# Fused decoder layer: casts and layer-norm scaling moved between engines, with a new instruction order

## The reference, cut to what matters

```
x = layernorm(x + linear_attention(x))        # 16 heads of 64; q' = exp(q Wqf), k' = exp(k Wkf), 32 features
                                              # out = q' (k'^T v) / (q' sum(k') + 1e-6), then Wproj
x = layernorm(x + cross_attention(x, ctx))    # 16 heads of 8, softmax over 64 keys, then Wo
x = layernorm(x + ffn(x))                     # h = gelu(x Wfc^T); layernorm(h) w + b; h Wproj^T
                                              # Wfc, Wproj ternary: sign(W/g) min(round(|W/g|), 1), g = mean|W|
```

## Time and profile before

| | us |
|---|---|
| median of 3 runs (lowest, highest) | 662.33 (658.06, 664.6) |
| the profiled execution | 662.33 |
| its span, first to last instruction | 660.5 |
| PE busy, of the span | 619.8 |
| DVE busy | 510.0 |
| ACT busy | 422.6 |
| POOL busy | 440.5 |

### The profile page before, as it was taken

How to read it: one execution, slowest core, us unless ns; L and a number is a source line. 1 busy time by engine, 2 the same in 40 slices (tenths; PEclk the granted TensorE clock), 3 DMA queues, 4 the chain that set the end, 5 groups by cost and what they waited for, 6 DMA issues and landing times.

```text
span 660.5 us, 31376 instructions
## 1 busy us (share of the span) xinstructions
PE 619.8 (94%) x13568; PEld 450.4 (68%) x13568; DVE 510.0 (77%) x1312; ACT 422.6 (64%) x746; POOL 440.5 (67%) x606
## 2 busy tenths in 40 slices
PE   9789999999999999999999999999999998996675
PEld 6567766677767867676677767777777676675453
DVE  2654657778888879798988878997888887689577
ACT  4445475776667576866667675867766675962353
POOL 3433245768787777877787877778687876666543
PEclk9989999999999999999999999999999999998598
DMA  8011314454454647455444546374544544522401
GB/s 340 25 35 42 98 44 103 71 131 74 139 77 101 121 76 161 77 141 72 135 74 124 96 99 138 76 158 64 143 71 135 87 101 97 100 51 74 112 3 48
DMA packets 116010, 64.63 MB, mean 98 GB/s; under 512 B 94305, under 2 KB 100834, under 8 KB 115746
## 3 DMA queue, kind: packets, MB, share of 16 engines
q1 hardware_dynamic: 115874, 62.64, 42.4%
HBM read 17.01 MB, written 4.19 MB: 32 GB/s over the span
## 4 chain that ended last, share of the span: by engine, by line
PE 77%; DMA 7%; DVE 6%; ACT 4%; POOL 3%; issue 2%; SPq 1%; POOLq 0%; DVEq 0%; ACTq 0%
PE bank L337 16%; PE bank L327 9%; PE bank L357 6%; PE bank L449 4%; DMA x2T<-x2s 4%; PE bank L284 3%; PE bank L318 3%; PE bank L435 2%; PE bank L295 2%; PE bank L483 2%; PE bank L276 2%; PE bank L278 2%; PE bank L277 2%; PE bank L286 2%; PE bank L285 2%; PE bank L306 2%
## 5 line engine op out<-in xcount | busy, mean ns | idle before, releaser
L337 PE MATMUL bank<-Mh,GT 128*32 128x128 f32 x4096 | 126.4, 275 | 0.0
L337 PEld LDWEIGHTS bank<-Mh,GT 128*32 128x32 f32 x4096 | 108.6, 110 | 20.4 <-issue 18.2
L543 ACT ACTIVATE Cb<-bank 128x512 f32<-128x512 f32 x99 | 57.6, 599 | 40.0 <-PE bank L337 39.6
L867 DVE TENSOR_REDUCE mx<-bank 128x8 f32<-128x512 f32 x128 | 79.1, 680 | 3.9 <-PE bank L414 3.9
L327 PE MATMUL bank<-kp,xs 64*128 64x512 f32 x256 | 81.5, 626 | 0.0
L674 ACT ACTIVATE gall<-bank 128x512 f32<-128x512 f32 x64 | 36.3, 594 | 70.1 <-PE bank L484 69.9
L543 ACT ACTIVATE GT<-bank 128x512 f32<-128x512 f32 x110 | 59.2, 607 | 31.4 <-PE bank L327 27.6
L647 ACT ACTIVATE PT<-bank 128x512 f32<-128x512 f32 x128 | 66.8, 639 | 8.5 <-PE bank L435 8.3
L1044 POOL TENSOR_TENSOR rstd<-ve,mhalf 128x4 f32<-128x4 f32 x64 | 66.1, 1033 | 5.3
L1105 POOL TENSOR_TENSOR gs<-gall,gs 128x512 f16<-128x512 f32 x56 | 65.0, 1160 | 4.5
L357 PE MATMUL bank<-Cb,qT 128*64 128x128 f32 x1024 | 59.4, 274 | 0.0
(11 more groups left out here) (193 smaller groups left out, 1559.9 us busy)
## 6 DMA issues: line engine op xcount, KB each, us to landing
pack<-Qh SPq DMA_DIRECT2D x64, 128.0 KB, 2.6
xT<-in_xT SPq DMA_DIRECT2D x16, 256.0 KB, 3.0
xs<-in_x_nat SPq DMA_DIRECT2D x16, 256.0 KB, 3.2
cxT<-in_cxT SPq DMA_DIRECT2D x16, 256.0 KB, 3.6
Kp<-Kh SPq DMA_DIRECT2D x32, 128.0 KB, 2.1
pack<-Ql SPq DMA_DIRECT2D x32, 128.0 KB, 2.6
out_y<-yo SPq DMA_DIRECT2D x15, 256.0 KB, 3.7
Kp<-Kl SPq DMA_DIRECT2D x16, 128.0 KB, 2.1
```

What stands on the lines that cost most here:

```text
L337: m = e.matmul(bk[32 * j:32 * j + 32, tile(g_)], GT[b % 4][:, tile(hh, 32)], Mh[:, tile(hh)], start=True, stop=True)
L543: e.activation(dst, src, ACT.Copy, scale=scale).then_inc(emptied(name, s, t)[0], 1)
L867: e.tensor_reduce(to, bank[uses["score", s, i][0]][:, :].rearrange("p (g b k) -> p g b k", g=2, b=4), AX.X, ALU.max).then_inc(emptied("sco ...
```

## The change

The second program does the same products. Four things differ.

- The high part of the gelu output (new word gh), of cT (cs) and of x1 (x1s) is cast by ACT; POOL still makes the low parts.
- ap1 and ap3, four scalings of 128x128 each, are done by POOL instead of DVE. For layer norm 1 the mean with its sign changed and the shift (nm, nmr) are no longer computed. DVE's aggregates of norms 1 to 3 wait for the scaling of the step before (`s_ln`).
- Of the G and C copies in the loop, ACT keeps 9 (g0, g1, g2, g6, c0, c4, c5, c6, c7) instead of 13, DVE does 7 (g3, g4, g5, g7, c1, c2, c3) instead of 3.
- HEAD, PERIOD and TAIL are ordered anew. HEAD starts with mh0 and mh1, so Wvp is the first transfer and the fillers stand behind mh; g6, g7, c4, c5 of step 0 belong to it. The number of periods, FILL, the buffers and the steps done by PE (flip, turn) are the same.

```
 HEAD = """
-small1 WkT wk zeros wq wb WqT k0 k1 loadx k2 Wvp k3 g0 bv mh0 g1+ g2 mh1 q0 nbeta split xb Wff q1 split@1 g3+ g4+ g5+ q2 small2 biasA gam qz c0+ c1+
-ks kst loadx@1 c2 c3+ q3 bias3 loadc bias2 xw sbar
+zeros mh0 mh1 wk wq k0 Wvp k1 WqT k2 q0 small1 wb nbeta WkT loadx g0+ g1+ g2+ Wff g3+ g4 g5 c0+ split split@1 c1 c2+ bv q1 q2 k3 biasA gam c3+ c4+ xb
+ks xw c5+ g6+ small2 g7+ kst q3 bias3 sbar loadc bias2 loadx@1 qz loadc@1 csplit
 PERIOD = """
-oturn1@3 qproj@2 c4+@1 ab1@2 c5+@1 dT@1 g6+@1 loadx@-1 g7@1 csplit@1 proj0@3 vproj@2 k0 ap3@5 k1 proj1@3 gl2@4 st2@3 k2 k3 bc@1 gl3@4 c6+@1 c7+@1
-ap2+@3 split@-1 loadc score0@2 g0+ ab2@3 g1+ g2+ down0@4 down1@4 score1@2 xb o@1 up0@3 rows@2 st1@1 up1@3 up2@3 gl0@3 down2@4 down3@4 st3@4 up3@3 c0
-c1 prob0@2 g3+ gl1@3 g4+ g5+ q0 ap1@1 x1s@1 kpack@1 stat@3 prob1@2 ks pv0@2 qpack@1 q1 oturn0@2 kproj@1 c2+ cs0@2 c3+ cs1@2 pv1@2 kst q2 q3
+cs1@3 c6+@1 loadx@-1 c7+@1 dT@1 kproj@1 down0@4 proj0@3 kpack@1 k0 proj1@3 st2@3 k1 k2 gl2@4 bc@1 gl3@4 k3 gh3@4 o@1 ab1@2 score0@2 score1@2 ap2+@3
+g0+ split@-1 g1+ g2+ st1@1 ks c0+ down1@4 q0 ap3@5 down2@4 ap1@1 up0@3 up1@3 ab2@3 down3@4 xb rows@2 up2@3 up3@3 gh0@3 x1s@1 g3 g4 gl0@3 gl1@3 qpack@1
+gh1@3 g5 c1 st3@4 c2 c3 prob0@2 csplit vproj@1 stat@3 q1 q2 prob1@2 pv0@2 oturn0@2 g6+ loadc@-1 cs0@2 kst gh2@3 g7 c4+ c5+ pv1@2 oturn1@2 q3 qproj@1
 TAIL = """
...
-st2@3 prob0@2 g7@1 prob1@2 st3@5 pv0@2 down0@4 ap2+@3 down1@4 bc@1 down2@4 ab2@3 pv1@2 oturn0@2 oturn1@2 c7+@1 gl0@3 o@1 kpack@1 st1@1 up0@3 down3@4
-stat@3 ap3@5 ab1@1 gl1@3 up1@3 st3@4 ap1@1 qpack@1 proj0@2 up2@3 proj1@2 up3@3 down0@3 st2@2 flip+@1 qproj@1 ap3@4 ap2+@2 down1@3 flip3@2 gl2@3
...
+bc@1 ab2@3 rows@2 down2@4 up0@3 ap3@5 up1@3 gl0@3 down3@4 up2@3 up3@3 stat@3 gh0@3 gh1@3 c7@1 o@1 st1@1 ap1@1 prob0@2 prob1@2 ab1@1 st3@4 gh2@3 pv0@2
+oturn0@2 flip+@1 pv1@2 oturn1@2 gl1@3 qproj@1 proj0@2 proj1@2 st2@2 down0@3 vproj@1 ap2+@2 down1@3 qpack@1 flip3@2 score0@1 gh3@3 gl2@3 tw@1 up0@2
...
@@ act_program
+            def ghi(s, t):
+                w.wait_ge(*emptied("up", s, t))
+                if t > 1:
+                    w.wait_ge(s_gT[t - 2], 16 * (s + 1))
+                elif s > 0:
+                    w.wait_ge(s_gT[t + 2], 16 * s)
+                e.activation(gs[t % 2][:, 0:512], g[t][:, :], ACT.Copy).then_inc(s_gh, 1)
...
+                elif name == "cs":
+                    chi(s, t)
+                elif name == "x1s":
+                    x1hi(s)
@@ dve_program, stats
+                if s > 0 and k != "4":
+                    w.wait_ge(s_ln[k], 4 * s)
...
-                elif not on_act and name in ("ap1", "ap2", "ap3"):
+                elif not on_act and name in ("ap2",):
@@ pool_program
-                if k == "3":
+                if k in ("1", "3"):
                     root(k, s)
                     return
...
+            def apply(k, s, x):
+                w.wait_ge(s_rstd[k], s + 1)
+                for t in range(4):
+                    e.tensor_scalar(x[:, tile(t)], x[:, tile(t)], mv[k][:, 2 * t:2 * t + 1], rstd[k][:, t:t + 1], ALU.subtract, ALU.mult).then_inc(s_ln[k], 1)
...
-                e.tensor_copy(x1s[:, 0:512], x1[s % 2][:, :]).then_inc(s_x1h, 1)
...
-                e.tensor_copy(gs[t % 2][:, 0:512], g[t][:, :]).then_inc(s_gh, 1)
...
-                e.tensor_copy(cs[tp][:, 0:256], cT[tp][:, :]).then_inc(s_ch, 1)
```

More of the change, by code:

```diff
@@ L43 @@
+gh1@3 g5 c1 st3@4 c2 c3 prob0@2 csplit vproj@1 stat@3 q1 q2 prob1@2 pv0@2 oturn0@2 g6+ loadc@-1 cs0@2 kst gh2@3 g7 c4+ c5+ pv1@2 oturn1@2 q3 qproj@1
 """
 TAIL = """
-tw@1 oturn1@4 qproj@3 vproj@3 dT@2 c4+@2 csplit@2 proj0@4 proj1@4 st2@4 down0@5 g6+@2 g7+@2 k0@1 gl2@5 bc@2 gl3@5 kproj@2 c5+@2 ap2+@4 score0@3 ab2@4
-c6+@2 c7+@2 score1@3 o@2 loadc@1 rows@3 vproj@2 q0@1 kpack@2 st1@2 k1@1 x1s@2 ab1@3 down1@5 xb@1 ap1@2 prob0@3 g0@1 g1+@1 k2@1 prob1@3 c0+@1 ap3@6
-qpack@2 pv0@3 k3@1 gl0@4 up0@4 down2@5 down3@5 qproj@2 q1@1 csplit@1 c1+@1 ab1@2 pv1@3 oturn0@3 gl1@4 oturn1@3 up1@4 g2+@1 g3+@1 g4+@1 g5+@1 cs0@3
@@ L48 @@
-g6+@1 up2@4 ks@1 kst@1 c2+@1 c3+@1 cs1@3 score0@2 gl2@4 up3@4 score1@2 kproj@1 q2@1 c4+@1 gl3@4 c5+@1 rows@2 q3@1 stat@4 proj0@3 proj1@3 c6+@1 dT@1
-st2@3 prob0@2 g7@1 prob1@2 st3@5 pv0@2 down0@4 ap2+@3 down1@4 bc@1 down2@4 ab2@3 pv1@2 oturn0@2 oturn1@2 c7+@1 gl0@3 o@1 kpack@1 st1@1 up0@3 down3@4
-stat@3 ap3@5 ab1@1 gl1@3 up1@3 st3@4 ap1@1 qpack@1 proj0@2 up2@3 proj1@2 up3@3 down0@3 st2@2 flip+@1 qproj@1 ap3@4 ap2+@2 down1@3 flip3@2 gl2@3
-vproj@1 score0@1 up0@2 gl3@3 ab2@2 score1@1 up1@2 down2@3 down3@3 rows@1 up2@2 up3@2 stat@2 prob0@1 prob1@1 turn0+@2 st3@3 pv0@1 oturn0@1 pv1@1
@@ L52 @@
-oturn1@1 turn1+@2 proj0@1 proj1@1 st2@1 ab2@1 down0@2 down1@2 turn2+@2 ap2+@1 turn3@2 down2@2 ap3@3 down3@2 flip3@1 up0@1 st3@2 stat@1 up1@1 up2@1
-turn0+@1 up3@1 turn1+@1 ap3@2 down0@1 turn2+@1 turn3+@1 down1@1 down2@1 down3@1 st3@1 ap3@1
+kpack@2 k0@1 ab1@3 proj0@4 c6+@2 c7@2 cs1@4 dT@2 gl2@5 k1@1 proj1@4 st2@4 kproj@2 vproj@2 bc@2 ap2+@4 k2@1 o@2 st1@2 gh3@5 g0+@1 ap3@6 gl3@5 ab2@4
+g1@1 k3@1 score0@3 score1@3 down0@5 up0@4 ks@1 gh0@4 ap1@2 up1@4 up2@4 kst@1 up3@4 down1@5 rows@3 x1s@2 gl0@4 gl1@4 c0+@1 ab1@2 down2@5 down3@5 gh1@4
@@ new lines @@
+stat@4 prob0@3 c1@1 qpack@2 prob1@3 g2@1 g3@1 pv0@3 oturn0@3 qproj@2 pv1@3 g4+@1 csplit@1 oturn1@3 cs0@3 g5+@1 gh2@4 gl2@4 cs1@3 c2@1 c3+@1 down0@4
+down1@4 gh3@4 q0@1 kpack@1 q1@1 proj0@3 gl3@4 proj1@3 st2@3 kproj@1 q2@1 q3@1 xb@1 score0@2 ap2+@3 dT@1 g6+@1 g7+@1 score1@2 c4+@1 c5+@1 st3@5 c6+@1
+bc@1 ab2@3 rows@2 down2@4 up0@3 ap3@5 up1@3 gl0@3 down3@4 up2@3 up3@3 stat@3 gh0@3 gh1@3 c7@1 o@1 st1@1 ap1@1 prob0@2 prob1@2 ab1@1 st3@4 gh2@3 pv0@2
+oturn0@2 flip+@1 pv1@2 oturn1@2 gl1@3 qproj@1 proj0@2 proj1@2 st2@2 down0@3 vproj@1 ap2+@2 down1@3 qpack@1 flip3@2 score0@1 gh3@3 gl2@3 tw@1 up0@2
@@ L54 @@
+gl3@3 up1@2 score1@1 up2@2 down2@3 up3@2 rows@1 ap3@4 ab2@2 turn0@2 down3@3 prob0@1 prob1@1 stat@2 pv0@1 turn1+@2 oturn0@1 pv1@1 turn2+@2 oturn1@1
+proj0@1 ap2+@1 down0@2 proj1@1 st2@1 down1@2 st3@3 ap3@3 ab2@1 turn3@2 down2@2 down3@2 flip3@1 up0@1 up1@1 up2@1 st3@2 up3@1 ap3@2 turn0+@1 turn1+@1
+stat@1 down0@1 turn2+@1 down1@1 turn3+@1 down2@1 down3@1 st3@1 ap3@1
 """
@@ L699, in act_program @@
                     {"kproj": kproj, "qproj": qproj, "vproj": vproj, "rows": rows, "flip3": flip3}[name](s)
-                elif name in ("k", "q", "prob", "up"):
-                    {"k": kexp, "q": qexp, "prob": prob, "up": up}[name](s, t)
+                elif name in ("k", "q", "prob", "up", "gh"):
+                    {"k": kexp, "q": qexp, "prob": prob, "up": up, "gh": ghi}[name](s, t)
                 elif on_act and name == "flip":
@@ L1131, in clo @@
                 w.wait_ge(s_cT, 2 * s + tp + 1)
-                if s > 0:
-                    w.wait_ge(*filled("proj", s - 1, tp))
-                e.tensor_copy(cs[tp][:, 0:256], cT[tp][:, :]).then_inc(s_ch, 1)
                 w.wait_ge(s_ch, 2 * s + tp + 1)
@@ L1138, in pool_program @@
             for name, s, t, on_act in PLAN:
+                if name in ("ap1", "ap3"):
+                    apply(name[2], s, {"ap1": x1, "ap2": x2, "ap3": yo}[name][s % 2])
                 if name == "zeros":
```

2 lines of the change are left out of this document (removed).

## The result

The changed kernel takes 697.52 us (median of 4, 695.73 to 698.64) against 663.47 for the kernel before on the same chip: ratio 1.0519, interval 1.0443 to 1.0597. The forecast was 654.6 with a range to 667, so sign and size were wrong. The runs of the kernel before lie between 658.06 and 666.83, so a difference under 1% says little without its interval. The profiled execution has a span of 694.3 us at a granted clock of 0.975, the clock of before.

A forecast was written before the change was run, and what follows sets the result against it. PE was taken to bound the loop (busy 365.19 of 367.10 us), latency the tail. Terms +3.5 -3.5 -3.5 -4.5 and +0.3 (last ap3 on POOL) gave -7.7 from 662.33: 654.6 us, range 646 to 667.

The forecast's parts named there:

- Engine loads: In the loop: DVE some -1.3 us a step, POOL -4.3 and +2.4 for eight scalings at 0.3, ACT +3.8 and -2.4.
- Term 1: The loop: waits for the transposed x2 (3.2 us) and 0.3 of small ones go; -3.5 us, ends -5 and +12.
- It fits by nothing: Loop, bc0's bank needed by o: only k3 (0.65 us) stands between, and DVE's first product takes 0.6.
- Rival C: Loop: ACT late at pv1, about 0.95 us in 13 steps; +12 us, so 666.6; chance 0.13.
- Term 2: The head: PE opens with Mh, waiting for Wvp, and POOL's memsets may hold DVE's constants; +3.5 us, ends -1 and +6.
- Rival A: The head: DVE isn't held beside POOL's memsets, so the head costs 0; 651.1 us; chance 0.22.
- Terms 3 and 4: The tail: -3.5 us from 541 to 595.3 us, and -4.5 in the last step from an earlier flip.
- rival B: The tail gives nothing, as step 14, sharing PE with step 15, is later now; 660.9 us; chance 0.20.
- term 3: From 541 to 595.3 us: longer distances shorten PE's waits, among them 1.6 for packed Q; -3.5 us, ends -5 and +2.
- The other-side rival: The one rival forecasting a slower kernel, by ACT late at pv1 in every step: 666.6 us, chance 0.13.

The follow-up runs named there:

- e8: Kernel before, with POOL instruction forms run alone behind the last store; 128x128 scaling with two per-partition operands 0.799 us; whole time of no interest.
- e1: Changed kernel with ap1 and ap3 both back on VectorE, the rest of the change kept: 677.65 us, ratio 1.0239 to the kernel before.
- e3: Changed kernel with ap1 alone back on VectorE, ap3 staying on POOL: 673.27 us, ratio 1.0165 to the kernel before.
- e16: e13 with st3 moved from behind c1 to behind oturn1 in PERIOD: 687.19 us, ratio 1.0357 to the kernel before.
- e18: e11 with ap2 moved ahead of c6 and c7 in PERIOD: 667.5 us, ratio 1.0069 to the kernel before.
- e10: Changed kernel with ap1 and ap3 on VectorE, POOL's memsets early, and c7 moved between k3 and o: 668.92 us, ratio 1.0085 to the kernel before.
- e5: Changed kernel with POOL's memsets of Q moved ahead of xb in HEAD: 691.37 us, ratio 1.0429 to the kernel before.
- e9: Changed kernel with ap1 moved directly ahead of ap3 in PERIOD, both on POOL: 712.55 us, ratio 1.0751 to the kernel before.
- e13: Changed kernel with ap1 where ap3 stood in PERIOD and ap3 behind rows, both on POOL: 696.27 us, ratio 1.0566 to the kernel before.
- e11: Kernel before with POOL's memsets of Q moved directly behind split in HEAD: 656.0 us, ratio 0.9902 to the kernel before.

## Why the prediction was wrong, term by term

**Engine loads, the step that failed.** "A scaling reads one tensor, so I take 0.3", with ends of 0.2 and 0.4 from the nearest rows. It measured 0.80. The rows bounded the wrong thing: no row showed a POOL instruction with per-partition operands on a wide tile, and the ends came from forms with none. The Trainium skill (GPSIMD Engine Reference, 4.1 Engine selection), weighed there, puts POOL near line rate on one input. For constants e8 agrees: 0.302 us, near the 0.274 that VectorE needs at the least for a 128x128 scaling. For the form used it disagrees, by a factor of 2.6. The text named 0.6 or more as a sign that it would be wrong, and gave it no price.

**"None nears 36 us, so this alone is neither gain nor loss."** The larger fault. I added up loads and never walked POOL's chain between o and x1s. The walk was possible from the rows: two groups of four in a row, 2.4 us at 0.3 each, 6.3 at 0.8. With one group the loop keeps the time that it has with none (e1 to e3), with two it loses 1.0 us a step; that was 12 us in the loop and 7 behind it. I checked ACT's queue for prob0 and prob1 only by ACT's own work, not by what ACT may stand for ahead of it.

**Term 1, the loop, -3.5; measured +19.8 up to o(13).** The x2T waits went, as said, though some came back in e16. No run shows what they are worth by themselves: e18 removed them in the old order and lost 11 us by what stood behind. Beyond the scalings' 12 us, some 8 come with the order, the casts and the copies together. "It fits by nothing" for o's bank was right, and PE waited 0.2 us a step there, which e10 took away for 0.17 a step; a place that fits by nothing should have had a price. Rival C named the right wait, PE's for ACT's PT, and a similar sum a step (0.95), but the wait came one product earlier, at prob1's banks, and not from ACT's own work, so that its nearness is luck.

**Term 2, the head, +3.5 (ends -1, +6); right.** k0 came at 16.3 (forecast 17.5), the stretched scaling ended with the memsets, sbar came at 43.3 (42.6), c6 at 45.7 (45), 5 us later than before for the same work; at o(1) it is 3.0. Two sizes were off and partly cancel: Mh took 3.7 us from its start to the fillers' instead of 5.2, the fillers 3.3 instead of 2.7. e5 shows the cause by taking it away: -6.2. Rival A is refuted for the change, and made true by e5. The Trainium skill (GPSIMD Engine Reference, 8. Key points), named there, has the contention. That DVE stands for 6.5 us is in the rows.

**Terms 3 and 4, the tail, -3.5 and -4.5; measured +6.3 from o(13) to o(15) and +4.6 behind.** The flip was to come within 6 us of o's end; its first transpose started 4.6 us behind it, its last ended 7.4 behind. POOL's timeline, and PE's behind it:

```profile
632.29 3.14 POOL L1078 TENSOR_SCALAR x<-x,mv,rstd 128x128 f32<-128x128 f32 x4
```

```profile
633.14 0.33 PE L364 MATMUL bank<-small,x 128*128 128x128 f32 x1 [0.85 <-POOL x L1078]
...
635.48 0.47 PE L364 MATMUL bank<-small,x 128*128 128x128 f32 x1 [0.45 <-POOL x L1078]
```

o ends at 628.5 and the flip at 635.9: 7.4 us, where it was 10.6. So 3.2 of the 4.5 came: the flip goes at the pace of the scalings, 3.14 us for four where 1.4 was forecast. But from the flip to the end it is 58.4 us instead of 50.5. The prediction took that chain as "nearly the same"; PE is busy 45.2 us behind o(15), not 41.6, with more products (730 recorded, not 557), at a mean clock of 0.80 as before (0.81), and it waits for PT (3.0), for ap2 on ACT (3.0) and for gT (1.9) there. So of the 4.6 us that this stretch has grown 3.6 are PE's busy time, and only 1.0 is idle. That was rival B's remark (step 14 is later now), taken at half its weight. In term 3, Q's pack wait fell from 1.6 to 0.5 as said, and PE waits 3.6 for PT and 1.8 for cs instead; its idle time from o(13) to o(15) grew from 5.1 to 8.3 us, where a gain of 3.5 was forecast. With the scalings on DVE (e1) the two stretches are +2.7 and +1.1: no gain without them either.

**The other-side rival.** The range closed at 667 since rival C was priced from ACT's work alone. What had a real chance to be slower was POOL's chain and the untested order, and neither had a case.

## What to carry to other kernels

Price an operation that moves to another engine by a row of its exact form there (operands from a tile or constants), or give it a wide end. Then walk, in program order, the chain from its producer to whatever stands behind its consumer in every in-order queue, DMA issue included; where two moved groups end up in series, price both together, since the cost of each alone may hide. In a schedule written out by hand, a wait that is removed often reappears elsewhere, as in e9, e13, e16, e18 and term 3. Look for memsets back to back beside small VectorE work: moving them cost one word and gave 1%.

## What the runs showed of the hardware

- On GpSimd, a 128x128 float32 tensor-scalar instruction takes 302 ns with constants, 606 with one per-partition operand and 799 with two (e8); the last is the same in the changed kernel beside VectorE and DMA work (797 to 802). With two, 128x4 takes 384 and 128x512 2080. A two-tensor product of 128x128 takes 400, and one of 128x512 with the statistics broadcast 1040, so that by an estimate two of those (subtract, multiply) would need some 2.1 us where the four scalings need 3.1. That form was not run in the kernel.
- VectorE's 128x2 scaling took 6.50 us beside GpSimd's back-to-back memsets and 1.23 with them moved away; in the kernel before, a 128x128 one fell from 6.45 to at most 1.30. In e5 and e11 the ones of over 1 us end within 0.1 us of the end of the GpSimd instruction beside them, which is no memset.
